# A four-layer attention and adapter kernel: maxima opened five slots sooner and spread evenly, adapter normalisation moved from VectorE to GpSimd, low-rank rows later

## The reference, cut to what matters

```python
def L0(seq1, seq2, len1, ...):            # 16 heads of 32
    q = heads((seq2 + b_self) @ Wq + bq)
    k = heads(concat([seq1 + b_prev, seq2 + b_self]) @ Wk + bk)
    v = heads(concat([seq1, seq2]) @ Wv + bv)
    score_prev = where(mask, q @ k[:512].T * SCALE, -inf)
    score_self = (q * k[512:]).sum(-1) * SCALE
    w = softmax(concat([score_prev, score_self]))
    return (w[..., :-1] @ v[:512] + w[..., -1:] * v[512:]) @ Wo + bo
def L1(x, f, e, stage):                   # one head of 512
    return softmax((x + e[stage]) @ f.T) @ f
def L2(h, lang, ...):                     # adapter, tables chosen by language
    a = relu(h @ W1[lang] + b1[lang]) @ W2[lang] + b2[lang]
    y = h + a
    n = (y - mean(y)) * rsqrt(var(y) + 1e-5)
    return n * gamma[lang] + beta[lang]
def L3(x, lang, ...):                     # low rank 16
    return (x @ A[lang].T) @ B[lang].T + emb[lang]
x = x + L0(x, f, lens); x = x + L1(x, f, ...); x = x + L2(x, ...); x = x + L3(x, ...)
```

## Time and profile before

| | us |
|---|---|
| median of 3 runs | 1279.25 (1278.84 to 1279.36) |
| profiled execution, its own time | 1278.37 |
| its span, first to last instruction | 1276.6 |
| PE busy | 1208.0 (95%) |
| DVE busy | 903.3 (71%) |
| ACT busy | 839.2 (66%) |
| POOL busy | 511.7 (40%) |

### The profile page before, as it was taken

How to read it: one execution, slowest core, us unless ns; L and a number is a source line. 1 busy time by engine, 2 the same in 40 slices (tenths; PEclk the granted TensorE clock), 3 DMA queues, 4 the chain that set the end, 5 groups by cost and what they waited for, 6 DMA issues and landing times.

```text
span 1276.6 us, 18385 instructions
## 1 busy us (share of the span) xinstructions
PE 1208.0 (95%) x6289; PEld 479.2 (38%) x6289; DVE 903.3 (71%) x1500; ACT 839.2 (66%) x1763; POOL 511.7 (40%) x445
## 2 busy tenths in 40 slices
PE   7999999999999999999989999999999999999995
PEld 4332443324442343323433244332443324433253
DVE  7876578766786658865598656986569855787556
ACT  5898348864588635985369853798438883388732
POOL 6505364044632366132751417605175053650212
PEclk9999999999999999999999999999999999999996
DMA  6304445136343273432633435424354154451110
GB/s 218 83 8 143 91 90 110 62 90 123 69 108 82 63 133 67 99 111 50 117 81 86 124 58 108 87 67 143 51 108 107 34 143 82 93 104 58 40 34 33
DMA packets 215322, 113.47 MB, mean 89 GB/s; under 512 B 166498, under 2 KB 189374, under 8 KB 215230
## 3 DMA queue, kind: packets, MB, share of 16 engines
q1 hardware_dynamic: 215168, 112.30, 39.0%
q10 hardware_dynamic: 62, 0.01, 0.0%
HBM read 40.81 MB, written 8.40 MB: 39 GB/s over the span
## 4 chain that ended last, share of the span: by engine, by line
PE 48%; ACT 23%; DVE 20%; issue 4%; DMA 1%; POOL 1%; SPq 1%; POOLq 0%; ACTq 0%; DVEq 0%
ACT banks L865 15%; PE bank L505 13%; PE banks L505 11%; PE banks L1539 9%; PE bank L1555 8%; DVE nmx L1147 7%; ACT big L921 3%; PE bank L1504 2%; DVE x L1105 2%; DVE prod L1136 2%; ACT bank L948 1%; PE banks L1467 1%; PE bank L1565 1%; SPq L684 1%; DVE tiles_in L1098 1%
## 5 line engine op out<-in xcount | busy, mean ns | idle before, releaser
L865 ACT ACTIVATE banks<-banks,nmx 128x512 f32<-128x512 f32 x512 | 342.6, 695 | 69.9 <-DVE nmx L1147 69.7
L1147 DVE TENSOR_REDUCE nmx<-banks 128x1 f32<-128x512 f32 x512 | 324.5, 682 | 22.3 <-PE banks L1467 21.8
L921 ACT ACTIVATE big<-banks 128x1024 f32<-128x1024 f32 x256 | 248.1, 1021 | 50.6 <-PE banks L1539 50.0
L505 PE MATMUL bank<-fT,w_hi 128*128 128x512 f16 x768 | 255.8, 379 | 0.6 <-DVE fT L1063 0.6
L1467 PE MATMUL banks<-KQ 97*128 97x512 f16 x512 | 196.6, 384 | 33.5 <-ACT banks L865 28.0
L625 POOL TENSOR_TENSOR x<-x,bo_rows 128x512 f32<-128x512 f32 x32 | 40.4, 1294 | 322.8 <-DMA x<-in_x_dram 322.8
L505 PE MATMUL bank<-fT,w_lo 128*128 128x512 f16 x384 | 145.4, 379 | 0.0
L1539 PE MATMUL banks<-KQ 98*128 98x512 f16 x512 | 142.0, 382 | 2.5 <-DVE q L1168 0.2
L542 POOL TENSOR_TENSOR split<-tiles_in,ones 128x512 f16<-128x512 f32 x56 | 61.5, 1098 | 200.8 <-DMA xT<-split 197.8
L1555 PE MATMUL bank<-big,V 128*32 128x512 f32 x1024 | 136.4, 605 | 0.0
L865 ACT ACTIVATION_READ_ACCUMULATOR banks<-banks,nmx 128x1 f32 x512 | 123.4, 241 | 0.0
(11 more groups left out here) (168 smaller groups left out, 1773.1 us busy)
## 6 DMA issues: line engine op xcount, KB each, us to landing
KQ<-half SPq DMA_DIRECT2D x384, 64.0 KB, 2.0
tiles_in<-in_x_dram SPq DMA_DIRECT2D x32, 256.0 KB, 8.0
x<-in_x_dram SPq DMA_DIRECT2D x8, 1024.0 KB, 5.4
out_dram<-x SPq DMA_DIRECT2D x32, 256.0 KB, 2.3
tiles_in<-in_fside_BxSxS_dram SPq DMA_DIRECT2D x28, 256.0 KB, 2.7
hT<-in_L_cond_W_dram SPq DMA_DIRECT2D x8, 256.0 KB, 3.9
w<-in_L_cond_W_dram SPq DMA_DIRECT2D x8, 256.0 KB, 4.0
b2r<-in_L_cond_b_dram SPq DMA_DIRECT2D x8, 256.0 KB, 4.4
```

Source lines behind the costliest of these rows:

```text
L505: mm = eng.matmul(out_ap, pairs[n][0], pairs[n][1], start=(first and n == 0), stop=(last and n == len(pairs) - 1))
L865: eng.activation(bank(step, i)[:, v, :], bank(step, i)[:, v, :], ACT.Exp, bias=nmx[:, t, h:h + 1], accum_out=esum[:, t, h:h + 1]).then_inc ...
L921: eng.activation(big[:, n % 2, 2 * u:2 * u + 2, :], bank(step)[:, :, :], ACT.Exp).then_inc(read(step), 1)
L1147: eng.tensor_reduce(nmx[:, t, h:h + 1], bank(step, i)[:, v, :], AX_X, ALU.max, negate=True).then_inc(max_done, 1)
```

## The change

The table `at` is written anew; the same steps stand at other slots, and a step `XG` is added. The adapter steps ahead of the maxima come one or two slots later, `NORM` at slot 32 (before 22), `X3` at 34, 36, 50 and 68 (before 40, 42, 46 and 50), `T3` at 42, 42, 60 and 70 (before 44, 44, 52 and 52), `LOW` at 76 and 88 (before 56 and 74), `LORA` at 80, 84, 92 and 96 (before 60, 64, 78 and 82).

The maxima of the seven stages no longer open by group. The first stands behind slot 30 and the others follow with one in 1.2 slots, five in six slots, up to slot 105 (before: 35 to 104); `MROW` comes at slot 106 and `SROW` at 112 (before 105 and 111). The stage ahead of the first sample keeps its order.

The Newton steps and the scaling of the seven stages run on POOL. Newton takes 14 instructions there, since POOL gets plain products in place of fused ones; the scaling is a product and a sum, both on POOL, ahead of the split of `X3`. The addition of beta is now `XG`: one tile between the halves of K0 and those of Q0, three behind those of Q0. V0 and V1 are evicted by DVE. The last sample's Newton stays on DVE, with 14 instructions a call in place of 11.

```diff
-              19: [("SCALE", 0)], 20: [("SCALE", 1), ("X3", 0)], 21: [("X3", 1)], 22: [("SCALE", 2), ("T3", 0), ("T3", 1)],
...
+              12: [("U", 3)], 16: [("NORM", 0)], 17: [("X3", 0)], 18: [("X3", 1)], 21: [("T3", 0), ("T3", 1)],
...
-    opens = [slots.index(("Q", g)) + OPEN[tail][g] for g in range(NG)]
+    opens = [slots.index(("Q", g)) + OPEN[g] for g in range(NG)]
+    due = [SPREAD_FROM + n * 6 // 5 if tail else opens[n // (4 * NT)] for n in range(H * NT)]
...
-        if maxima and i >= opens[maxima[0][1]]:
+        if maxima and i >= due[-len(maxima)]:
             out.append(maxima.pop(0))
...
-OPEN = ((32, 26, 26, 26), (24, 24, 24, 24))
+OPEN = (32, 26, 26, 26)
+SPREAD_FROM = 30
...
+V_BY_DVE = (0, 1)
...
-NEWTON = 11
+NEWTON = 14
...
+        def norms_of(eng, n, head, i):
...
+            eng.wait_ge(sq_done, i * NT + at.stop)
+            eng.tensor_scalar(var, st[:, at, 2], 1.0 / D, EPS, ALU.mult, ALU.add).then_inc(newton, 1)
+            eng.wait_ge(newton, base + 1)
+            eng.tensor_scalar(r_int, si[:, at, 3], -0.5, 0x5F3759DF, ALU.mult, ALU.add).then_inc(newton, 1)
+            for k in range(base + 2, base + NEWTON, 4):
+                eng.wait_ge(newton, k)
+                eng.tensor_tensor(c, r, r, ALU.mult).then_inc(newton, 1)
+                eng.wait_ge(newton, k + 1)
+                eng.tensor_tensor(c, c, var, ALU.mult).then_inc(newton, 1)
+                eng.wait_ge(newton, k + 2)
+                eng.tensor_scalar(c, c, -0.5, 1.5, ALU.mult, ALU.add).then_inc(newton, 1)
+                eng.wait_ge(newton, k + 3)
+                eng.tensor_tensor(r, r, c, ALU.mult).then_inc(newton, 1)
...
-                        if head and t == NT - 1:
-                            add_beta(range(NT), head, i)
+                    elif step[0] == "XG":
+                        add_beta(step[1:2], head, i)
...
+                    elif step[0] == "NORM":
+                        norms_of(eng, step[1], head, i)
                     elif step[0] == "X3":
                         t = step[1]
+                        eng.wait_ge(newton, (i + 1) * NEWTON)
+                        eng.wait_ge(normed, i * NT + t + 1)
+                        eng.tensor_scalar(yb[:, t, :], yb[:, t, :], st[:, t, 4:5], None, ALU.mult).then_inc(scaled, 1)
+                        eng.wait_ge(scaled, i * NT + t + 1)
+                        eng.wait_ge(xg_done, i * NT + t + 1)
+                        eng.tensor_tensor(x1[:, t, :], yb[:, t, :], x1[:, t, :], ALU.add).then_inc(x3_done, 1)
                         eng.wait_ge(x3_done, i * NT + t + 1)
...
-                    elif kind == "V":
+                    elif kind == "V" and step[1] not in V_BY_DVE:
...
-                    elif kind == "NORM":
-                        norms_of(step[1], head, i)
+                    elif kind == "V" and step[1] in V_BY_DVE:
+                        wait_full(eng, step, b)
+                        eng.tensor_scalar(V[:, step[1], :], bank(step, i)[:, :], 1.0 / WS, None, ALU.mult
+                                          ).then_inc(read(step, i), 1)
+                    elif kind == "NORM" and not head:
+                        norms_of(eng, step[1], head, i)
```

More of the change, by code:

```diff
@@ L87, in order_mid @@
     if tail:
-        at = {4: [("HID", 0)], 6: [("ADP", 0), ("HID", 1)], 7: [("ADP", 1), ("SQ", 0)], 8: [("ADP", 2), ("SQ", 1), ("U", 0)],
[3 rows of a table removed]
-              28: [("LOW", 0)], 30: [("LORA", 0)], 32: [("LORA", 1)], 37: [("LOW", 1)], 39: [("LORA", 2)], 41: [("LORA", 3)]}
+        at = {4: [("XG", 0)], 5: [("HID", 0)], 7: [("XG", 1), ("ADP", 0), ("HID", 1)], 8: [("XG", 2), ("ADP", 1), ("SQ", 0)],
[3 rows of a table added]
+              38: [("LOW", 0)], 40: [("LORA", 0)], 42: [("LORA", 1)], 44: [("LOW", 1)], 46: [("LORA", 2)], 48: [("LORA", 3)]}
         adapters = [at.get(n, []) for n in range(max(at) + 1)]
@@ L216, in order_last @@
                ("LOW", 3), ("LORA", 3)])
-ADAPTERS = ("X2", "X2T", "HID", "ADP", "SQ", "U", "NORM", "SCALE", "X3", "T3", "X3T", "LOW", "LORA")
+ADAPTERS = ("X2", "XG", "X2T", "HID", "ADP", "SQ", "U", "NORM", "SCALE", "X3", "T3", "X3T", "LOW", "LORA")
 def tokens(step, head):
@@ L483, in build_program @@
         normed = sem("normed")
+        scaled = sem("scaled")
         x3_done = sem("x3_done")
@@ L507, in hi_lo @@
             return mm
+        def norms_of(eng, n, head, i):
+            tiles = NT if head else NT // 2
+            at = slice(n * tiles, n * tiles + tiles)
+            si = st[:, :, :].bitcast(I32)
+            var, r, c, r_int = st[:, at, 3], st[:, at, 4], st[:, at, 5], si[:, at, 4]
+            base = (i + n) * NEWTON
+            eng.wait_ge(sq_done, i * NT + at.stop)
[11 more added lines that the diff above has]
+                eng.tensor_tensor(r, r, c, ALU.mult).then_inc(newton, 1)
         @block.gpsimd
@@ L1074, in add_values @@
                                          in1=x1[:, t, :], op0=ALU.mult, op1=ALU.add).then_inc(read(step, i), 1)
[L1076 to L1093, removed]
             def centre(t, i):
```

## The result

The changed kernel took 1295.84 us (median of 4 runs, 1294.41 to 1296.06) against 1279.23 of the kernel before: ratio 1.0129, 95% interval [1.0116, 1.0142], so 1.3% slower. The forecast was 1265, its range 1247 to 1287. The profiled execution took 1295.76 us, its span 1293.9.

A forecast was written before the change was run, and what follows sets the result against it. PE, busy 95%, was taken as the bound, losing 8 us a `mid` stage behind DVE, then ACT. 1278.4 - 10.9 - 3.5 + 0.6 = 1264.6, plus 0.9 for the median: 1265.5, said as 1265; range 1247 to 1287.

The forecast's parts named there:

- The new wait: PE's first block of group 2 would wait 4.3 us for stack 2, in each of seven stages.
- The friction of the second part: From the first maximum of group 2 to MROW, 2.2 us on top of PE's 26.4 us of work.
- POOL's chain: Work between Q1's halves and stack 2's issue: Newton 3.0, two scaled X3 tiles 9.3, halves of K2 and Q2 4.5 us.
- The scaling product, 0.9: On POOL, a 128 x 512 tile times a column, ahead of each X3 split: 0.9 us, between 0.52 and 1.04.
- Newton, 3.0: 14 dependent instructions on POOL behind Q1's halves, 0.21 us each, 3.0 us in all, between 1.4 and 6.0.
- the 14 that were to be won: The whole run's forecast gain: 10.9 us in seven stages and 3.5 of stack waits, less 0.6 lost.
- The 3.5 us for the waits of group 0: Of PE's 4.9 us of waits for stacks, 3.5 would go, since one beta addition instead of four precedes the halves.
- a gain of 1.6 a stage: From first maximum through MROW and the slots behind it, each steady stage would win 1.6 us, 10.9 in seven.
- small terms: V0 and V1 evictions on DVE, late LORA stores (nothing), and the last sample's longer NORM, 0.6 us lost.
- POOL decides, and it is slower: Rival, chance 0.18: 0.43 us a Newton instruction and 1.04 a scaling delay stack 2 by 3.3 us; 1288.
- The second part stays bound by ACT: Rival, chance 0.15: from group 2 to MROW, ACT's unchanged work gives 4.4 us of friction; 1281.
- POOL is quicker: Rival, chance 0.17: POOL's work ahead of stack 2 is 2.4 us shorter, a stage wins 4.0; 1248.

The follow-up runs named there:

- e1: The changed kernel with POOL's scaling as a product of two tensors (column broadcast) in place of tensor_scalar: 1295.56 us.
- e3: The changed kernel with 28 matmuls of unused result on PE in each steady stage, ahead of the block that waits: 1285.59 us.
- e10: The changed kernel with e1's product, e2's late X3 tiles and X3 tile 0 also behind Q2's halves: 1267.25 us.
- e2: The changed kernel with X3 tile 1 behind Q2's halves, tiles 2 and 3 behind Q3's, their transposes later: 1248.48 us.
- e9: The changed kernel with e1's product and 24 matmuls of unused result ahead of group 2: 1278.73 us.
- e8: The changed kernel with Newton alone back on DVE, scaling still on POOL: 1277.91 us.

## Why the prediction was wrong

What it removed went as said: DVE's small instructions and scalings left the maxima, PE's waits for exponentials fell by 18.5 us, and the waits of group 0 for its stack are gone.

The new wait was named right, with its place and count (seven, at the first block of group 2) and its parts: PE stands there 24.5 us after its first maximum (24.1 said), and the stack is ready 9.2 us behind the halves (9.2 said). The friction of the second part came to 2.0 in the stage shown (30.17 - 26.4 - 1.8 for the clock) where 2.2 was said. The wait itself was 6.4 us a stage where 4.3 was said, and 44.5 in all where 26 to 33 was said.

**The step that failed is the price of POOL's chain**, 16.8 us said and 19.1 measured. The scaling product, 0.9 between the bounds 0.52 and 1.04, took 1.56: outside both. The upper bound was a two-tensor instruction; in the same place POOL took 1.56 us with a column as scalar operand and 1.04 with two tensors (e1). That is 1.3 us over two tiles. Newton, 3.0, took 4.1: 14 instructions of 0.20 with 0.08 between. The bounds of 1.4 and 6.0 held it, but the MEMSET of 0.10 that the value leaned on was the wrong row: each of the 14 took twice that. This step alone is enough for the wrong sign: 2.3 us in seven stages are 16, more than the 14 that were to be won, and with the clock held (e3) the kernel is at 1285.6, still 0.5% slower than before.

**The term that was left out is the clock.** The wait was priced at its length alone. Behind 6.46 us of it the trace shows 1.8 us more, and e3 shows by experiment some 1.5 a stage. The Trainium skill says so in "TensorE: Matmul & The Clock Gate", section "Loop structure matters more than you think": a long wait for a DMA between matmuls leaves the next ones at the low clock. The trace agrees: the granted clock is 0.50 behind 6.46 us of idling. A fall of the clock should have been among the rivals.

**One gain was counted twice.** The 3.5 us for the waits of group 0 stood beside a gain of 1.6 a stage, read from a stage that had no such wait. Yet the stages with such a wait were hardly longer: from MROW to MROW the kernel before takes 153.7 to 155.2 us, and the one with the longest wait, 1.85 us, is 0.7 longer than the stage read. From the first maximum to MROW the stage read takes 55.9 us and the seven average 55.5, so the others begin later and end alike.

The ledger: from first maximum to MROW 57.0 us were said for a stage, and seven average 61.3 (arrival +0.4, wait 6.4 for 4.3, clock 1.8): 4.3 x 7 = 30. With the 3.5 counted twice that makes 33, where 31.2 us lie between 1264.6 and 1295.76; the surplus of about 2 us is in small terms, which no run took apart.

Of the rivals, "POOL decides, and it is slower" had the mechanism and the sign, but not the condition: Newton stayed at 0.29 us an instruction, under the 0.36 given, and the scaling added the rest of the 2.0 us a stage from which it decides. Its 1288 lacks the clock as well. "The second part stays bound by ACT" fell: ACT is busy 24.8 of 30.2 us there (25.1 of 26.9 before), its exponentials are 15% of the chain of waits from group 2 to MROW (76% before), and MROW waits less. "POOL is quicker" fell with the 0.20 and the 1.56.

## What to carry to other kernels

When work moves to an engine that has room on average, look at what is queued behind it there in the order of the program: one tile of X3 behind the critical halves instead of ahead of them, with the next tiles later still, was worth 47 us, more than the whole change was expected to win. What is put behind must still be in time for its own reader (e10). Take as upper bound for an unshown instruction the nearest row of another kind and then a wider one, because a form with fewer tensor operands need not be cheaper. A wait of TensorE behind which the clock falls costs more than its length, and shortening it in part may give nothing (e1) until it is nearly gone (e2) or filled (e3, e9).

## What the runs showed of the hardware that was not expected

- On POOL, a 128 x 512 fp32 product with a column as scalar operand took 1.56 us; as a product of two tensors with the same column broadcast, 1.04; the addition of two full tiles beside it 1.26.
- Fourteen dependent instructions on 128 x 4 values took 0.285 us each on POOL, 0.20 recorded and 0.08 between.
- PE working through a wait of 6.5 us on matmuls without use made the kernel 10 us faster than letting it idle.
- A wait shorter by 1.1 us left the kernel's time unchanged: the half clock then covered 5.7 us of work instead of 3.6.
- The length of a single wait did not tell whether the clock fell: in e8 a wait of PE for stack 2 of 2.51 us was followed by half clock and one of 3.10 us was not, and in e2 one of 1.87 us was.
